# First expert weights issued ahead of the barrier, and one wait at the expert border removed

## Chip, cores and metric
The kernel runs on all 8 cores of one Trainium2 chip, each with one of the 8 sequences of the batch; the cores do not communicate. The metric is the device time in microseconds (us) of the slowest core.

## What is computed
One transformer layer with a parallel attention and expert branch, on x of shape 8 x 2048 x 1024 (float32):

```python
xn = layernorm(x)
x = x + local_attention(xn, w_qkv, b_qkv, w_proj, b_proj) + moe(xn, ...)

# local attention: 16 heads of 64, windows of 256 queries, keys of the
# window and of 128 positions on either side, softmax, projection
# moe: 8 experts, hidden size 2048, the best 2 of 8 weighted by softmax
h0 = einsum('td,ehd->eth', xt, w0) + b0
h1 = einsum('td,ehd->eth', xt, w1) + b1
out_all = einsum('eth,edh->etd', h0 * silu(h1), w2) + b2
out = (softmax(top_v) * take(out_all, top_i)).sum()
```

Every expert is computed for every token; a gate weight of zero drops the ones that are not chosen.

## The kernel before
Each core holds its 2048 tokens transposed: the 1024 features lie on partitions as 8 tiles `xn[dt]` of 128 x 2048 in bf16, the tokens run along the free dimension. All engines' instruction streams are written out by hand: `step` emits an instruction that may increment its engine's counter (`ct` TensorE, `cv` VectorE, `cs` ScalarE, `cg` GpSimd), `dma` emits a transfer that increments a counter of its own by 16, and `rec.wait` lets an engine wait until a counter has reached a value. `rec.wait` leaves out a wait on a value that the engine has already waited for. `barrier()` (L206) makes every engine drain, increment a counter of its own, and wait for those of the other four.

The stages come one after the other. Layer norm statistics, normalisation and gate; a barrier; the q, k and v projections; a barrier; the attention in 128 steps; a barrier; the transposes of the attention output (L660) and its projection (L681, evicted to the bf16 sum tiles `SUM[dt]` at L688). Then comes the b2 stage (L692 to L706): 32 rounds, each of one TensorE matmul of 8 x 128 by 8 x 512 (L699: the expert biases b2 times the gate weights) into one of two PSUM banks and one VectorE add into SUM (L704). Each matmul waits for the add of the round before it. After a further barrier (L711) the expert stage begins.

In the expert stage (L733 on) a loop runs over the 8 experts `e`. Its first part loops over 16 tiles `ht` of 128 hidden features, and for each over 4 token chunks `tc` of 512: eight matmuls with w0 (L756), eight with w1 (L762), the Silu on ScalarE (L771) and the product on VectorE into `act[ht]` (L777). PSUM banks 0 to 5 are used in turn as three pairs, so a chunk waits for the eviction three chunks before. The second part multiplies `act` by W2 (16 matmuls for each of 32 outputs, L798) into banks 6 and 7; VectorE multiplies by the gate weights `gwb` into `tmpb` (L803) and adds into SUM (L805).

The weights arrive from GpSimd's DMA queue (POOL in the profile), which converts them from float32 to bf16. `emit_slice_dma(e, ht)` loads the w0 and w1 slices of one `ht` (256 KB each) into one of four slots. For e = 0 the first four are issued before the loop's first matmul, followed by W2T of expert 0 (4 MB) and `gwb`. From then on a slot's next load is issued when its matmuls are done, so the first four slices of the next expert go out during the last four `ht` of this one. W2T of the next expert is issued after the last W2 matmul, its `gwb` after the last L805.

The memory for the slots, for W2T and for gwb overlaps `AO`, the attention output before its transposition, which the transposes read. `act` overlaps the transposed attention output and the projection weights.

At the top of every `ht` TensorE waits for its two slices and, where e > 0, for the last L805 of the expert before. `last_act`, which TensorE waits for between the two parts, covers all evictions of the PSUM pairs, and VectorE itself waits for the last W2 matmul before it writes `act` again. Behind the loop the final stage adds x and stores the result (L837).

Of the kernel before, what the change touches and what calls it, by code (L numbers as in the profile page):

```python
# [20 lines left out]
NDT = D // 128  # L21
NTT = T // 128
NTC = T // 512
# [33 lines left out]
def build_program(debug_upto=None):  # L57
# [8 lines left out]
    w2T_in = nc.dram_tensor("w2T", [NE, HF, D], F32, kind="ExternalInput")  # L66
# [9 lines left out]
    gw_hbm = nc.dram_tensor("gw_scratch", [NE, T], F32)  # L76
# [3 lines left out]
    def sb(name, shape, dtype, off):  # L80
        return nc.alloc_sbuf_tensor_at(name, shape, dtype, offset=base + off)
# [69 lines left out]
    W2T_sb = sb("W2T", [128, NHT * D], BF16, OB + 96 * KB)  # L151
    w0sl = [sb(f"w0sl{i}", [128, NDT * 128], BF16, OB + 128 * KB + i * 2 * KB) for i in range(4)]
    w1sl = [sb(f"w1sl{i}", [128, NDT * 128], BF16, OB + 136 * KB + i * 2 * KB) for i in range(4)]
    gwb_sb = sb("gwb", [128, T], BF16, OB + 144 * KB)
# [11 lines left out]
    rec = Rec()  # L166
    ct = Ctr(stack, nc, "ct")
    cv = Ctr(stack, nc, "cv")
# [9 lines left out]
    dgww = Ctr(stack, nc, "dgww")  # L178
    dw0 = [Ctr(stack, nc, f"dw0{i}") for i in range(4)]
    dw1 = [Ctr(stack, nc, f"dw1{i}") for i in range(4)]  # L180
    dw2 = Ctr(stack, nc, "dw2")
    dgwb = Ctr(stack, nc, "dgwb")
# [3 lines left out]
    def dma(eng, ctr, out_ap, in_ap):  # L186
        ctr.n += 16
        v = ctr.n
        sem = ctr.sem
        rec.emit(eng, lambda E, o_=out_ap, i_=in_ap, s=sem: E.dma_start(out=o_, in_=i_).then_inc(s, 16))  # L190
        return v
# [14 lines left out]
    def barrier():  # L206
        for e in Rec.ENGINES:
            c = BCTR[e]
            c.n += 1
            sem = c.sem  # L210
            rec.emit(e, lambda E, s=sem: E.drain().then_inc(s, 1))  # L211
        snap = {e: BCTR[e].n for e in Rec.ENGINES}
        for e in Rec.ENGINES:
            for f in Rec.ENGINES:
                if f != e:
                    rec.wait(e, BCTR[f], snap[f])
# [9 lines left out]
    def finalize():  # L226
        def run(E, name):
            for kind, f in rec.ops[name]:
                if kind == "op_dr":
                    E.drain()  # L230
                f(E)

        with nc.Block() as block:
            @block.tensor
            def _(t):
                run(t, "tensor")

            @block.vector
            def _(v):
                run(v, "vector")  # L240

            @block.scalar
            def _(s):
                run(s, "scalar")

            @block.sync
            def _(s):
                run(s, "sync")

            @block.gpsimd  # L250
            def _(g):
                run(g, "gpsimd")

        stack.close()
        return nc
# [210 lines left out]
    gwT_hbm_done = dma("sync", dgww, gw_hbm[:], gwT_sb[:])  # L466
# [203 lines left out]
    proj_mm = {}  # L670
# [37 lines left out]
    if debug_upto == "p3":  # L708
        finish_debug(SUM)
        return finalize()  # L710
    barrier()  # L711

    w2_loaded = 0
    gwb_loaded = 0
# [3 lines left out]
    w2_evac_d = {}  # L718
    b_last_mm = 0

    def emit_slice_dma(e, ht):
        slot = ht % 4
        if (e, ht - 4) in h_mm_done:
            rec.wait("gpsimd", ct, h_mm_done[(e, ht - 4)])
        elif e > 0 and ht < 4:
            rec.wait("gpsimd", ct, h_mm_done[(e - 1, NHT - 4 + ht)])
        a = dma("gpsimd", dw0[slot], w0sl[slot][:],
                w0T_in[e][:, ht * 128:(ht + 1) * 128].rearrange("(a p) o -> p a o", p=128))
        b = dma("gpsimd", dw1[slot], w1sl[slot][:],
                w1T_in[e][:, ht * 128:(ht + 1) * 128].rearrange("(a p) o -> p a o", p=128))  # L730
        sl_loaded[(e, ht)] = (slot, a, b)

    for e in range(NE):  # L733
        if e == 0:
            for _h in range(4):
                emit_slice_dma(0, _h)
            rec.wait("gpsimd", dgww, gwT_hbm_done)
            w2_loaded = dma("gpsimd", dw2, W2T_sb[:],
                            w2T_in[0][:, :].rearrange("(a p) d -> p a d", p=128))
            gwb_loaded = dma("gpsimd", dgwb, gwb_sb[:], gw_hbm[0][None, :].partition_broadcast(128))  # L740

        for ht in range(NHT):
            slot = ht % 4
            bcol = e * 16 + ht
            _sl, _a, _b = sl_loaded[(e, ht)]
            rec.wait("tensor", dw0[_sl], _a)
            rec.wait("tensor", dw1[_sl], _b)
            if e > 0:
                rec.wait("tensor", cv, w2_evac_d[(e - 1, NTC * NDT - 1)])
            for tc in range(NTC):  # L750
                i = ht * NTC + tc
                par = i % 3
                if i >= 3:
                    rec.wait("tensor", cv, act_evac[(e, i - 3)])
                for dt in range(NDT):
                    step("tensor", lambda t, s=slot, dt=dt, tc=tc, par=par: t.matmul(  # L756
                        pb[par * 2][:], w0sl[s][:, dt * 128:(dt + 1) * 128],
                        xn[dt][:, tc * 512:(tc + 1) * 512],
                        start=(dt == 0), stop=(dt == NDT - 1)))
                for dt in range(NDT):  # L760
                    last = (dt == NDT - 1)
                    h_mm_done[(e, ht)] = step("tensor", lambda t, s=slot, dt=dt, tc=tc, par=par: t.matmul(  # L762
                        pb[par * 2 + 1][:], w1sl[s][:, dt * 128:(dt + 1) * 128],
                        xn[dt][:, tc * 512:(tc + 1) * 512],
                        start=(dt == 0), stop=(dt == NDT - 1)), ct if last else None) \
                        or h_mm_done.get((e, ht), 0)
                hm = h_mm_done[(e, ht)]
                rec.wait("scalar", ct, hm)
                if i >= 3:
                    rec.wait("scalar", cv, act_evac[(e, i - 3)])  # L770
                sil_done = step("scalar", lambda s, par=par, bcol=bcol: s.activation(  # L771
                    out=silb[par][:], in_=pb[par * 2 + 1][:], func=AF.Silu,
                    bias=b1cols[:, bcol:bcol + 1], scale=1.0), cs)
                rec.wait("vector", cs, sil_done)
                if e > 0:
                    rec.wait("vector", ct, b_last_mm)
                act_evac[(e, i)] = step("vector", lambda v, ht=ht, tc=tc, par=par, bcol=bcol: v.scalar_tensor_tensor(  # L777
                    out=act[ht][:, tc * 512:(tc + 1) * 512], in0=pb[par * 2][:],
                    scalar=b0cols[:, bcol:bcol + 1], in1=silb[par][:],
                    op0=ALU.add, op1=ALU.mult), cv)  # L780
            if ht + 4 < NHT:
                emit_slice_dma(e, ht + 4)
            elif e + 1 < NE:
                emit_slice_dma(e + 1, ht + 4 - NHT)

        rec.wait("tensor", dw2, w2_loaded)
        rec.wait("vector", dgwb, gwb_loaded)
        last_act = act_evac[(e, NHT * NTC - 1)]
        rec.wait("tensor", cv, last_act)
        for tc in range(NTC):  # L790
            for dt in range(NDT):
                j = tc * NDT + dt
                bk = 6 + j % 2
                if j >= 2:
                    rec.wait("tensor", cv, w2_evac_d[(e, j - 2)])
                for ht in range(NHT):
                    last = (ht == NHT - 1)
                    b_last_mm = step("tensor", lambda t, ht=ht, dt=dt, tc=tc, bk=bk: t.matmul(  # L798
                        pb[bk][:], W2T_sb[:, ht * D + dt * 128:ht * D + dt * 128 + 128],
                        act[ht][:, tc * 512:(tc + 1) * 512],  # L800
                        start=(ht == 0), stop=(ht == NHT - 1)), ct if last else None) or b_last_mm
                rec.wait("vector", ct, b_last_mm)
                step("vector", lambda v, tc=tc, bk=bk, j=j: v.tensor_tensor(  # L803
                    tmpb[0][:], pb[bk][:], gwb_sb[:, tc * 512:(tc + 1) * 512], ALU.mult), dr=True)
                w2_evac_d[(e, j)] = step("vector", lambda v, dt=dt, tc=tc, j=j: v.tensor_tensor(  # L805
                    SUM[dt][:, tc * 512:(tc + 1) * 512], SUM[dt][:, tc * 512:(tc + 1) * 512],
                    tmpb[0][:], ALU.add), cv, dr=True)
        if e + 1 < NE:
            rec.wait("gpsimd", ct, b_last_mm)
            w2_loaded = dma("gpsimd", dw2, W2T_sb[:],  # L810
                            w2T_in[e + 1][:, :].rearrange("(a p) d -> p a d", p=128))
            rec.wait("gpsimd", cv, w2_evac_d[(e, NTC * NDT - 1)])
            gwb_loaded = dma("gpsimd", dgwb, gwb_sb[:],
                             gw_hbm[e + 1][None, :].partition_broadcast(128))
# [67 lines left out]
```

## Time and profile before
| | us |
|---|---|
| median of two runs | 3448.32 |
| the two runs | 3435.47 and 3461.17 |
| profiled execution | 3438.49 |
| its span (slowest core) | 3436.5 |
| spans of the 8 cores | 3423.9 to 3436.5 |

| engine | busy us | share of the span |
|---|---|---|
| TensorE (PE) | 3191.1 | 93% |
| VectorE (DVE) | 1066.8 | 31% |
| ScalarE (ACT) | 525.3 | 15% |
| GpSimd (POOL) | 272.8 | 8% |

The span runs from a core's first to its last instruction; the time of the execution holds a little more. PE stands for TensorE's matmuls, PEld for its weight loads, and an engine's name with a q (DVEq, POOLq) for its sequencer, which handles waits and semaphores. Matmuls are pipelined and their ends are modelled, so the time of a single one overlaps the next one's. In a row of the timeline, what stands in brackets is how long the engine was idle before and who ended that. L190 is the line of the helper `dma`. The granted clock is a share of TensorE's full 2.4 GHz.

### The profile page before, as it was taken

How to read it: one execution, taken by the hardware profiler on the slowest of the kernel's cores; microseconds unless marked ns; L12 is line 12 of the kernel's file. 1: busy time of each engine (PE TensorE's matmuls, PEld its weight loads, DVE VectorE, ACT ScalarE, POOL GpSimd, SP SyncE). 2: the span in 40 equal slices, each digit the busy share in tenths (PEclk: the TensorE clock that was granted, in tenths of full speed). 3: DMA queues.
4: the chain of work that ended last, by engine and by line, in shares of the span. 5: the costliest groups of instructions: out<-in, count | busy, mean ns of one | idle time of the engine just before them, and what ended most of it. 6: DMA issues, size and time to landing. Idle time of an engine off the chain costs nothing.

```text
span 3436.5 us, 38188 instructions; the slowest of 8 cores (3423.9 to 3436.5 us)
## 1 busy us (share of the span) xinstructions
PE 3191.1 (93%) x15278; PEld 1484.8 (43%) x15278; DVE 1066.8 (31%) x1816; ACT 525.3 (15%) x665; POOL 272.8 (8%) x303
## 2 busy tenths in 40 slices
PE   3689998689999999999999999999999999999993
PEld 0634554234444444444444444444444444444441
DVE  3533455412242223222322232233223322332233
ACT  2200473012101210111011001100120011001100
POOL 0010000021101110110011001100110011001001
PEclk6589656799999999999999999999999999999997
DMA  3233001084306330642163225313441443144204
GB/s 119 86 36 39 1 1 26 0 104 42 32 1 86 37 31 1 89 40 25 16 77 37 25 31 68 37 19 46 53 41 16 65 40 38 13 68 40 22 25 171
DMA packets 310573, 150.15 MB, mean 44 GB/s; under 512 B 285296, under 2 KB 287728, under 8 KB 306296
## 3 DMA queue, kind: packets, MB, share of 16 engines
q0 software_dynamic: 304016, 113.84, 29.4%
q10 hardware_dynamic: 2304, 16.78, 1.5%
q1 hardware_dynamic: 4080, 17.09, 1.4%
q8 instruction: 125, 2.05, 0.2%
q14 instruction: 48, 0.39, 0.0%
HBM read 252.53 MB, written 8.45 MB: 76 GB/s over the span
## 4 chain that ended last, share of the span: by engine, by line
PE 91%; DVE 3%; DMA 3%; issue 1%; ACT 1%; DVEq 1%; ACTq 0%; SPq 0%; POOL 0%; POOLq 0%
PE pd L756 26%; PE pb L798 26%; PE pd L762 26%; PE pd L585 3%; PE pd L499 2%; DMA xs<-xT 2%; PE pb L615 2%; PE pd L532 2%; PE pd L681 1%; PE pb L499 1%; DVE SUM L704 1%; PE pd L396 1%; PE pb L699 1%; DVEq L230 0%; PE pb L681 0%
## 5 line engine op out<-in xcount | busy, mean ns | idle before, releaser
L756 PE MATMUL pd<-xn,w0sl 128*128 128x512 bf16 x4096 | 969.0, 379 | 23.9 <-DVE SUM L805 12.3
L762 PE MATMUL pd<-xn,w1sl 128*128 128x512 bf16 x4096 | 967.6, 379 | 0.0
L798 PE MATMUL pb<-act,W2T 128*128 128x512 bf16 x4096 | 885.3, 379 | 14.7 <-DVE act L777 14.7
L777 DVE SCALAR_TENSOR_TENSOR act<-pd,b0cols,sil 128x512 bf16<-128x512 f32 x512 | 384.5, 751 | 1411.7 <-ACT sil L771 1411.7
L771 ACT ACTIVATE sil<-pd,b1cols 128x512 bf16<-128x512 f32 x512 | 351.9, 687 | 2213.2 <-PE pd L762 2213.2
L756 PEld LDWEIGHTS pd<-xn,w0sl 128*128 128x128 bf16 x4096 | 400.5, 98 | 510.0 <-issue 29.3
L798 PEld LDWEIGHTS pb<-act,W2T 128*128 128x128 bf16 x4096 | 400.2, 98 | 499.8 <-issue 18.4
L762 PEld LDWEIGHTS pd<-xn,w1sl 128*128 128x128 bf16 x4096 | 400.8, 98 | 483.4 <-issue 0.3
L803 DVE TENSOR_TENSOR tmpb<-pb,gwb 128x512 f32<-128x512 f32 x256 | 177.1, 692 | 525.5 <-PE pb L798 525.5
L190 POOL DMA_DIRECT2D w0sl<-w0T x128 | 112.1, 876 | 1640.3 <-PE pd L762 1511.9
L805 DVE TENSOR_TENSOR SUM<-SUM,tmpb 128x512 bf16<-128x512 bf16 x256 | 180.4, 705 | 19.6 <-issue 0.9
L598 ACT ACTIVATE exp<-pd,c_shift 128x1024 bf16<-128x1024 f32 (+1 forms) x128 | 135.7, 1062 | 252.1 <-PE pd L585 252.1
L585 PE MATMUL pd<-qT,kT 64*128 64x256 bf16 x480 | 123.4, 407 | 1.9 <-POOLq L211 1.9
L190 POOL DMA_DIRECT2D w1sl<-w1T x128 | 113.1, 883 | 0.0
L499 PE MATMUL pd<-xn,qksl 128*128 128x512 bf16 x384 | 95.5, 386 | 7.4 <-DMA qksl<-wqkvT 7.4
L615 PEld LDWEIGHTS pb<-V,exp 128*128 128x128 bf16 x960 | 55.3, 126 | 56.5 <-issue 56.5
L627 DVE TENSOR_SCALAR AO<-pb,rc 128x64 bf16<-128x64 f32 x256 | 72.6, 284 | 21.1 <-issue 1.4
L615 PE MATMUL pb<-V,exp 128*128 128x65 bf16 x960 | 73.9, 241 | 3.8 <-ACT exp L598 2.3
L190 POOL DMA_DIRECT2D W2T<-w2T x8 | 9.2, 1152 | 775.4 <-PE pb L798 775.4
L499 PEld LDWEIGHTS pd<-xn,qksl 128*128 128x128 bf16 x384 | 38.0, 99 | 54.6 <-issue 10.8
L625 DVE RECIPROCAL rc<-pb 128x1 f32<-128x1 f32 x256 | 41.6, 162 | 64.2 <-PE pb L615 64.1
L585 PEld LDWEIGHTS pd<-qT,kT 64*128 64x128 bf16 x480 | 49.0, 125 | 28.7 <-issue 2.4
(84 smaller groups left out, 743.7 us busy)
## 6 DMA issues: line engine op xcount, KB each, us to landing
w0sl<-w0T POOLq DMA_DIRECT2D x128, 256.0 KB, 4.4
w1sl<-w1T POOLq DMA_DIRECT2D x128, 256.0 KB, 5.2
W2T<-w2T POOLq DMA_DIRECT2D x8, 4096.0 KB, 30.8
xs<-xT SPq DMA_DIRECT2D x12, 1024.0 KB, 7.0
xs<-xT ACTq DMA_DIRECT2D x12, 1024.0 KB, 7.2
qksl<-wqkvT POOLq DMA_DIRECT2D x16, 256.0 KB, 4.8
gwb<-gw_scratch POOLq DMA_DIRECT2D x8, 512.0 KB, 32.2
outT<-ob ACTq DMA_DIRECT2D x4, 1024.0 KB, 5.0
```

The source lines that it names most:

```text
L190: rec.emit(eng, lambda E, o_=out_ap, i_=in_ap, s=sem: E.dma_start(out=o_, in_=i_).then_inc(s, 16))
L499: qk_mm_done[ot] = step("tensor", lambda t, s=slot, bs=bs, dt=dt, c=c: t.matmul(pb[bs + c][:], qksl[s][:, dt * 128:(dt + 1) * 128], xn[dt] ...
L585: dd = step("tensor", lambda t, d=dst, pt=pt, po=po, kt=kt, g=g: t.matmul(d, kT[pt][po:po + 64, kt * 128:(kt + 1) * 128], qT[pt][po:po + 6 ...
L598: exp_done_l[it] = step("scalar", lambda s, e=par, par=par, nk=nk: s.activation(out=expb[e][:, 0:nk * 256], in_=pd[par][:, 0:nk * 256], fu ...
L615: av_done = step("tensor", lambda t, e=par, j=j, qi=qi, kt=kt, abk=abk, h=h, nk=nk: t.matmul(pb[abk][:, qi * 65:qi * 65 + 65], expb[e][:, ...
L756: step("tensor", lambda t, s=slot, dt=dt, tc=tc, par=par: t.matmul(pb[par * 2][:], w0sl[s][:, dt * 128:(dt + 1) * 128], xn[dt][:, tc * 512 ...
L762: h_mm_done[(e, ht)] = step("tensor", lambda t, s=slot, dt=dt, tc=tc, par=par: t.matmul(pb[par * 2 + 1][:], w1sl[s][:, dt * 128:(dt + 1) * ...
L771: sil_done = step("scalar", lambda s, par=par, bcol=bcol: s.activation(out=silb[par][:], in_=pb[par * 2 + 1][:], func=AF.Silu, bias=b1cols ...
L777: act_evac[(e, i)] = step("vector", lambda v, ht=ht, tc=tc, par=par, bcol=bcol: v.scalar_tensor_tensor(out=act[ht][:, tc * 512:(tc + 1) * ...
L798: b_last_mm = step("tensor", lambda t, ht=ht, dt=dt, tc=tc, bk=bk: t.matmul(pb[bk][:], W2T_sb[:, ht * D + dt * 128:ht * D + dt * 128 + 128 ...
L803: step("vector", lambda v, tc=tc, bk=bk, j=j: v.tensor_tensor(tmpb[0][:], pb[bk][:], gwb_sb[:, tc * 512:(tc + 1) * 512], ALU.mult), dr=True)
L805: w2_evac_d[(e, j)] = step("vector", lambda v, dt=dt, tc=tc, j=j: v.tensor_tensor(SUM[dt][:, tc * 512:(tc + 1) * 512], SUM[dt][:, tc * 512 ...
```

## The change
Two edits. The first moves the barrier that stands between the b2 stage and the expert stage behind the first ten weight transfers, and takes these out of the loop over the experts. GpSimd now waits for the last projection matmul before it issues them; all transposes, which read the memory that they overwrite, come before that matmul. The second deletes TensorE's wait for the last L805 of the expert before.

```diff
     if debug_upto == "p3":
         finish_debug(SUM)
         return finalize()
-    barrier()
...
+    rec.wait("gpsimd", ct, proj_mm[NDT - 1])
+    for _h in range(4):
+        emit_slice_dma(0, _h)
+    rec.wait("gpsimd", dgww, gwT_hbm_done)
+    w2_loaded = dma("gpsimd", dw2, W2T_sb[:],
+                    w2T_in[0][:, :].rearrange("(a p) d -> p a d", p=128))
+    gwb_loaded = dma("gpsimd", dgwb, gwb_sb[:], gw_hbm[0][None, :].partition_broadcast(128))
+    barrier()
+
     for e in range(NE):
-        if e == 0:
-            for _h in range(4):
-                emit_slice_dma(0, _h)
-            rec.wait("gpsimd", dgww, gwT_hbm_done)
-            w2_loaded = dma("gpsimd", dw2, W2T_sb[:],
-                            w2T_in[0][:, :].rearrange("(a p) d -> p a d", p=128))
-            gwb_loaded = dma("gpsimd", dgwb, gwb_sb[:], gw_hbm[0][None, :].partition_broadcast(128))
-
         for ht in range(NHT):
...
             rec.wait("tensor", dw0[_sl], _a)
             rec.wait("tensor", dw1[_sl], _b)
-            if e > 0:
-                rec.wait("tensor", cv, w2_evac_d[(e - 1, NTC * NDT - 1)])
             for tc in range(NTC):
```

## Rows read from the trace of the kernel before

**Rows 1.** The cores: span and mean granted TensorE clock, the two longest.
```profile
core 3: 3435.6 us, clock 0.930
...
core 5: 3436.5 us, clock 0.931
```

**Rows 2.** The chain that ended last, by line, share of the span (page, part 4).
```profile
PE pd L756 26%; PE pb L798 26%; PE pd L762 26%; PE pd L585 3%; PE pd L499 2%; DMA xs<-xT 2%; PE pb L615 2%; PE pd L532 2%; PE pd L681 1%; PE pb L499 1%; DVE SUM L704 1%; PE pd L396 1%; PE pb L699 1%; DVEq L230 0%; PE pb L681 0%
```

**Rows 3.** Busy time by stretch, core 5: length, engines (instructions), clock, DMA share, GB/s.
```profile
640.00:690.00 50.00, 18.33 (x32) 3.18 (x32) 22.56 (x33) 0.00 (x0) 0.00 (x0) 0.52 0.00 0
690.00:700.00 10.00, 0.00 (x0) 0.00 (x0) 0.00 (x0) 0.00 (x0) 8.68 (x10) 0.50 0.81 68
700.00:704.00 4.00, 3.55 (x10) 1.34 (x11) 0.00 (x0) 0.00 (x0) 0.00 (x0) 0.58 1.45 133
704.00:925.00 221.00, 219.16 (x1016) 99.25 (x1015) 48.07 (x64) 45.31 (x65) 27.68 (x32) 1.00 0.56 62
925.00:1037.30 112.30, 110.55 (x512) 49.91 (x511) 44.31 (x64) 0.00 (x0) 1.49 (x2) 1.00 0.05 5
```

**Rows 4.** Waits of core 5: engine line <- releaser: total us, times, longest.
```profile
PE pd L756 <- DVE SUM L805: 12.3, 7, 1.8
PE pd L756 <- DMA w1sl<-w1T: 11.6, 1, 11.6
```

**Rows 5.** Timeline of core 5, 630 to 726 us: start, us, engine, line, operation.
```profile
637.13 0.59 PE L681 MATMUL pb<-AOT,wp 128*128 128x512 bf16 x2
...
641.37 0.69 DVE L704 TENSOR_TENSOR SUM<-SUM,pb 128x512 bf16<-128x512 bf16 x1 [0.80 <-PE pb L699]
...
688.98 0.69 DVE L704 TENSOR_TENSOR SUM<-SUM,pb 128x512 bf16<-128x512 bf16 x1 [0.83 <-PE pb L699]
690.38 0.87 POOL L190 DMA_DIRECT2D w0sl<-w0T  x1 [128.41 <-DVEq L211]
...
698.42 0.63 POOL L190 DMA_DIRECT2D gwb<-gw_scratch  x1
...
700.45 3.31 PE L756 MATMUL pd<-xn,w0sl 128*128 128x512 bf16 x8 [11.58 <-DMA w1sl<-w1T]
```

**Rows 6.** Timeline of core 5 at the first border between experts.
```profile
1029.78 5.78 PE L798 MATMUL pb<-act,W2T 128*128 128x512 bf16 x26
...
1036.11 1.15 POOL L190 DMA_DIRECT2D W2T<-w2T  x1 [110.77 <-PE pb L798]
1036.48 0.69 DVE L805 TENSOR_TENSOR SUM<-SUM,tmpb 128x512 bf16<-128x512 bf16 x1
...
1037.32 1.89 PE L756 MATMUL pd<-xn,w0sl 128*128 128x512 bf16 x8 [1.76 <-DVE SUM L805]
```

**Rows 7.** Chain that ended last, core 5, 636 to 712 us: start, us, what.
```profile
689.67 0.06 DVEq L211
...
691.24 9.08 DMA w1sl<-w1T
...
703.76 1.73 PE pd L762 x8
```

**Rows 8.** The same chain on core 3.
```profile
689.71 7.86 DMA w1sl<-w1T
...
697.70 3.57 PE pd L756 x8
701.28 2.65 PE pd L762 x8
```

**Rows 9.** DMA issues of core 5, 690 to 746 us, KB each, us to landing.
```profile
W2T<-w2T POOLq DMA_DIRECT2D x1, 4096.0 KB, 45.6
...
gwb<-gw_scratch POOLq DMA_DIRECT2D x1, 512.0 KB, 47.1
```

**Rows 10.** Timeline of core 5 after the last W2 matmul.
```profile
3383.86 4.07 POOL L837 TENSOR_TENSOR ob<-SUM,xs 128x2048 f32<-128x2048 bf16 x1 [165.68 <-PE pb L798]
3384.57 3.91 DVE L805 TENSOR_TENSOR SUM<-SUM,tmpb 128x512 bf16<-128x512 bf16 x1
```

## Prediction

> **What bounds the kernel now.** I read the cores first. Core 5 is the slowest with 3436.5 us and core 3 is next with 3435.6 [rows 1]. The profiled execution took 3438.49 us, so 1.99 us lie outside the span. All sums below are made against that execution. The runs shown are 3435.47 and 3461.17 us with a median of 3448.32, so the profiled execution lies near the lower one and 9.8 us under the median.
>
> Then the chain that ended last, by line: the three expert matmul lines L756, L762 and L798 hold 26% each [rows 2]. TensorE is the bound. From 704 us on it is busy 219.16 of 221 us and its granted clock is 1.00, the 2.4 GHz level [rows 3]. Inside the expert stage there is thus little to win except where TensorE stands still. There are two such places that this change can touch, and the waits of the chain name both: 11.6 us once, for the DMA into w1sl, and 12.3 us in 7 waits, for the add of L805 [rows 4].
>
> The first place is the seam between the b2 additions and the experts. On core 5 the last projection matmul ends near 637.72 (637.13 + 0.59). From then to 689.67 TensorE and VectorE take turns, one small matmul and one L704 add at a time: 32 adds, the first at 641.37, the last at 688.98, 1.54 us apart. Only when the barrier has passed does POOL issue its ten DMAs, the first at 690.38, the last at 698.42. The first expert matmul starts at 700.45 [rows 5]. During the b2 stage no DMA moves anything: its share is 0.00 [rows 3].
>
> The second place is each of the 7 borders between experts: after the last W2 matmul, VectorE multiplies (L803) and adds (L805), and only then does L756 of the next expert start, at 1037.32 [rows 6].
>
> **The change, step by step.**
>
> *The DMAs move ahead of the barrier.* POOL now waits for the last projection matmul in place of VectorE's last b2 add. The second wait that moves with them, for the gate weights stored to HBM long before, costs nothing. Four pairs of slices, W2T and gwb, ten issues in all, then start about 0.6 us after 637.72, at 638.3; the 0.6 us is taken from 690.38 - 689.73, release to first issue [rows 5, 7]. They occupy POOL for 8.68 us (in the stretch 690 to 700, as now [rows 3]), so until about 647. The first pair, which landed 9.08 us after the second issue began [rows 7], is there by about 648.5, some 41 us before it is wanted. The load is fully hidden behind the b2 stage; if that cover were gone, the 11.6 us would be back.
>
> What is behind the DMAs on POOL's queue is only the barrier, which POOL reaches at about 647, and VectorE at 689.7. So VectorE still ends the barrier last. TensorE then finds its slices. VectorE's barrier semaphore is at 689.73 and POOL's release needs a few steps of 0.06 us; from data landed (700.32) to matmul took 0.13 us [rows 5, 7]. I take 0.5 us from VectorE's end, so the first L756 stands at 690.2. The gain on core 5 is 700.45 - 690.2 = 10.3 us (10.0 to 10.6). On core 3 the second issue began 1.53 us earlier (689.71 against 691.24) and the first L756 at 697.70 [rows 7, 8], so its barrier ends at 688.14 + 0.5 and its gain is 9.1 us.
>
> The clock at the start: the b2 stage has 0.52, near the 1.2 GHz level, though TensorE is busy for 18.33 of 50 us. The first 4 us of the experts have 0.58 [rows 3], so the first eight matmuls take 3.31 us, and those after them 1.73. After the change the stage before is the same, so I price this start as now. Core 3 needed 2.65 us for its second eight [rows 8], which bounds the uncertainty at about 0.9 us either way.
>
> W2T and gwb land 45.6 and 47.1 us after issue [rows 9]; they are first read at 925, now and then. Earlier landing is worth nothing there. Slices of ht = 4 and later, which now queue behind W2T, only get more room.
>
> *The wait for L805 goes.* Eight full matmuls take 1.73 us of the chain [rows 7], so starts are 0.216 us apart, and the last of the 26 that begin at 1029.78 starts at 1029.78 + 25 x 0.216 = 1035.18. The next starts at 1037.32 [rows 6]: 2.14 us where 0.216 would do. That is 1.92 us at each of 7 borders, 13.5 us. The lower bound is nothing, if another wait takes its place. What would be late next? The next expert's first four slice pairs wait only for this expert's last L762, so they have the 110 us of the W2 matmuls [rows 3] to land. The banks of par 0 to 2 were emptied before W2 began. The fourth tile's wait for act comes three tiles (6 x 1.73 = 10.4 us) later, and VectorE is through with L805 at 1037.17, before the first tile's own matmuls (two times 1.73 us from 1035.4) have ended. So nothing is late, and I take 13.5.
>
> *Does POOL's work disturb the b2 stage?* Before, POOL was idle in it, so no row shows an L704 beside a DMA issue. The nearest: an L805, which has two operands in SBUF, ran 0.69 us from 1036.48 while POOL issued W2T from 1036.11 to 1037.26 [rows 6]; that price is nothing. The farthest: the last L805 took 3.91 us in place of 0.69, beside a POOL tensor operation that began at 3383.86 and lasted 4.07 [rows 10]. So POOL can hold VectorE up. If each of the ten issues did so in full, the b2 stage would grow by 8.7 us. I take nothing, since the first row has the same kind of POOL instruction.
>
> The Trainium skill, "SBUF — State Buffer", section "SBUF: two separate sides", says that VectorE and GpSimd share a port pair under an exclusive lock, which the first to start keeps for its whole instruction. The last L805 agrees with it, the one beside W2T does not show it for a DMA issue. By the lock applied to issues the sum would be 8.7 us worse, by the row nothing.
>
> *Sum.* Core 5: 3436.5 - 10.3 - 13.5 = 3412.7. Core 3: 3435.6 - 9.1 - 13.5 = 3413.0, which makes it the slowest by a little. With 1.99 outside the span: **3415 us**, 23.5 us or 0.7% less than the profiled execution. The end of the kernel (stores and adds) moves with it unchanged.
>
> **The rivals.**
>
> *POOL's barrier waits for its transfers.* The barrier begins with a drain, and no row shows POOL draining with transfers of its own under way. If the drain held until gwb landed, then by the present course (first issue 690.38, gwb at 698.42 + 47.1 = 745.5, 55.1 us together [rows 5, 9]) POOL would be free at 693.4, and the first L756 would start at 693.9: a gain of 6.5 in place of 10.3, 3419 us. It decides only above 52 us from first issue to last landing. Against it: POOL issues the next DMA without waiting for the one before [rows 5].
>
> *VectorE is held up in the b2 stage*, as priced above: 3415 + 8.7 = 3424 us. The row beside W2T speaks against it.
>
> *The change doesn't do what it says at one place.* If another wait takes the place of L805, 3415 + 13.5 = 3428.5; if the first slices still come late, 3415 + 10.3 = 3425. I found no candidate for either.
>
> *Slower: TensorE's clock gives back more than is won.* The place is the expert stage, 700 to 3384 us. Its matmuls scale with the clock, so each 0.01 of granted clock costs about 27 us there; at a loss of 0.009 the 23.5 us are gone, and at 0.99 in place of 1.00 the time would be 3442. For it: the same kernel has a run that is 25.7 us longer than the other, so something of this size does occur, though no row shows what; and the change takes away the only pauses of the stage. Against it: the pauses are 1.76 us [rows 6] in some 333 (221.0 + 112.3), and the stretch of 221 us without one has 1.00 [rows 3].
>
> **How the numbers follow.** Both gains as worked out: 0.74, time 3415, its own range 3411 to 3419. Drain: 0.07, at 3419. VectorE held up: 0.06, at 3424. One part without effect: 0.07, at 3425 to 3428.5. Clock: 0.06, at 3442. The runs before lie 3 us below and 23 us above the profiled one, so one that catches the upper spread may read 3438. The range goes from 3408 (the likeliest's low end less the 3 us) to 3436: it takes in all but the clock case and part of that spread, about 0.15. A difference of 2%, 69 us, is about what a measurement of this kernel can tell from no change. No case wins 69 us, as both idle times together are 24, so faster has 0.01. The clock would have to fall by over 0.03 for slower, 0.02. Within 2%: 0.97.
>
> **What the profile after would show.** If right: POOL's first w0sl issue near 638, no wait of L756 for a DMA, first L756 within 1 us of the last L704, no wait of L756 for L805, and starts 0.22 us apart at the borders. L704 keeps 0.69 us and its rounds 1.54. A longer L704 or longer rounds would show VectorE held up. A POOL semaphore as the last releaser of the barrier, well behind VectorE's end, would show the drain. A granted clock under 1.00 inside the experts would show the last rival. The prediction is wrong if TensorE, freed at either place, stands still in front of something I did not list.

## The result

The kernel after takes 3419.73 us against 3440.49 before (medians of 18 and 17 runs). The ratio of the comparable runs is 0.9929, with a 95% interval of 0.9911 to 0.9948: a gain of 0.5 to 0.9%, clear of noise and within 2%. The profiled execution took 3416.62 us. Some runs of both kernels were much longer, with a lower granted clock on one die or both; they are in these two medians, and in no ratio or comparison of runs below, which use the others, called comparable. Thirteen runs of each kernel are left. Those after lie between 3414.8 and 3422.0 us; eleven of those before lie between 3435.5 and 3443.6, and two apart, at 3461.17 and 3470.83. Without these two the ratio of the means is 0.9941.

The spans of the two longest cores after, which answer to [rows 1] (core: span and mean granted clock):

```profile
core 3: 3414.2 us, clock 0.930
...
core 7: 3414.5 us, clock 0.930
```

The waits of core 7 on TensorE's first expert line are short now. Of the two rows in [rows 4] neither is left; one new wait has come:

```profile
PE pd L756 <- POOLq L211: 5.0, 1, 5.0
```

POOLq L211 is GpSimd's sequencer in the barrier's drain, the instruction that `barrier()` begins with on every engine. The wait of 11.6 us for w1sl has become one of 5.0 us for POOL, and the 12.3 us for L805 have gone without a successor. The seam on core 7, which answers to [rows 5] (timeline: start, us, engine, line, operation):

```profile
632.05 0.87 POOL L190 DMA_DIRECT2D w0sl<-w0T  x1 [76.29 <-PE pb L681]
...
640.10 0.63 POOL L190 DMA_DIRECT2D gwb<-gw_scratch  x1
...
682.75 0.69 DVE L704 TENSOR_TENSOR SUM<-SUM,pb 128x512 bf16<-128x512 bf16 x1 [0.83 <-PE pb L699]
...
687.61 3.20 PE L756 MATMUL pd<-xn,w0sl 128*128 128x512 bf16 x8 [4.97 <-POOLq L211]
```

The issues begin behind the projection, as forecast, and end about 640.7. The last b2 add ends at 683.44, but the first expert matmul starts 4.17 us later. The chain of the same core shows what held it, which answers to [rows 7] (start, us, what):

```profile
636.42 50.81 POOLq L211
687.23 0.38 issue
687.61 3.20 PE pd L756 x8
690.81 1.73 PE pd L762 x8
```

POOL's sequencer is on the chain until 687.23. The last of its transfers to land, gwb, took 46.6 us from 640.10, so it landed at about 686.7, half a microsecond before (DMA issues of core 7, KB each, us to landing; they answer to [rows 9]):

```profile
W2T<-w2T POOLq DMA_DIRECT2D x1, 4096.0 KB, 45.3
...
gwb<-gw_scratch POOLq DMA_DIRECT2D x1, 512.0 KB, 46.6
```

On core 2 of the same execution gwb was issued at 637.95 and took 42.4 us, so it landed at 680.35, before the last add's end at 681.07. There VectorE is the last releaser, and the first expert matmul starts 0.72 us after the add's end:

```profile
681.79 3.57 PE L756 MATMUL pd<-xn,w0sl 128*128 128x512 bf16 x8 [1.52 <-DVEq L211]
```

On five of the eight cores POOL is the last releaser, as on core 7, and on three VectorE, as on core 2.

The border between experts on core 7, which answers to [rows 6]. The 59 matmuls begin at 1009.70, so the last starts at 1009.70 + 58 x 0.216 = 1022.23, and L756 follows 0.21 us later, without a gap:

```profile
1009.70 12.90 PE L798 MATMUL pb<-act,W2T 128*128 128x512 bf16 x59
1022.44 1.89 PE L756 MATMUL pd<-xn,w0sl 128*128 128x512 bf16 x8
```

Busy time by stretch on core 7, which answers to [rows 3] (length, busy us of PE, PEld, DVE, ACT and POOL with instructions, granted clock, DMA share, GB/s):

```profile
634.00:683.40 49.40, 18.35 (x32) 3.17 (x32) 22.28 (x33) 0.00 (x0) 6.73 (x8) 0.52 1.10 136
683.40:687.60 4.20, 0.00 (x0) 0.02 (x1) 0.03 (x1) 0.00 (x0) 0.00 (x0) 0.50 0.14 27
687.60:692.00 4.40, 4.39 (x15) 1.74 (x16) 0.00 (x0) 0.00 (x0) 0.00 (x0) 0.69 0.00 0
692.00:908.00 216.00, 216.00 (x1003) 97.91 (x1002) 46.95 (x63) 44.58 (x64) 26.24 (x30) 1.00 0.38 37
...
692.00:3362.00 2670.00, 2650.52 (x12275) 1200.25 (x12273) 741.75 (x1025) 353.14 (x513) 232.68 (x263) 1.00 0.34 38
```

The transfers now lie under the b2 stage (136 GB/s where there was 0), the stage itself has the same clock of 0.52, the first expert matmuls start at a lowered clock as before (0.69 over 4.4 us), and from 692 to 908 TensorE is busy all the time. Its clock is 1.00 there and over the whole expert stage.

To see where the time went, I cut every core's span at four points of its timeline and took the mean over the 8 cores: the first L704 starts; the last L704 ends; the first expert matmul starts; the last L803 starts. "Seam" is the third stretch, "tail" what follows the last point. Each row comes from one profiled execution of a kernel.

| us, mean of 8 cores | to the b2 stage | b2 stage | seam | experts | tail |
|---|---|---|---|---|---|
| before | 636.43 | 48.21 | 8.78 | 2683.84 | 52.63 |
| after | 634.55 | 48.18 | 2.10 | 2670.34 | 53.66 |
| move_only | 638.08 | 48.14 | 1.44 | 2683.75 | 54.62 |
| wait_only | 636.27 | 48.13 | 9.02 | 2670.42 | 54.12 |
| slices_ahead | 637.52 | 48.14 | 0.73 | 2670.28 | 54.77 |
| signal_first | 635.41 | 48.21 | 0.74 | 2670.09 | 55.32 |
| after_b2two | 637.19 | 24.45 | 24.42 | 2670.62 | 54.58 |
| half_w2_b2two | 636.11 | 24.41 | 11.61 | 2670.68 | 52.61 |
| signal_first_b2two | 636.51 | 24.45 | 0.73 | 2670.14 | 53.79 |

The change won 13.50 us in the experts and 6.68 in the seam. The first and the last column, whose work no edit touches, differ by up to 3.5 and 2.7 us between these executions; on single cores the b2 stage begins anywhere from 630 to 644 us. That is noise for the question here, and it is as large as some of the terms. So differences of a few us are read from the seam and the experts, and the times only say how they add up.

### The profile page after: what moved, and what is told of

Same layout as the page of the kernel before. It is cut to its first block, busy times and chain, and to the rows that moved or that the text cites. A ratio compares the mean times of both kernels' runs of the same rounds, so it can differ in the third digit from the quotient of the medians.

```text
span 3414.5 us, 38182 instructions; the slowest of 8 cores (3402.2 to 3414.5 us)
## 1 busy us (share of the span) xinstructions
PE 3190.9 (93%) x15278; PEld 1485.5 (44%) x15278; DVE 1066.5 (31%) x1816; ACT 525.2 (15%) x665; POOL 272.8 (8%) x303
## 4 chain that ended last, share of the span: by engine, by line
PE 91%; DVE 2%; DMA 2%; POOLq 1%; issue 1%; ACT 1%; DVEq 1%; POOL 0%; ACTq 0%; SPq 0%
PE pd L756 26%; PE pb L798 26%; PE pd L762 26%; PE pd L585 3%; PE pd L499 2%; DMA xs<-xT 2%; PE pb L615 2%; PE pd L532 2%; POOLq L211 1%; PE pd L681 1%; PE pb L499 1%; PE pd L396 1%; DVEq L230 0%; PE pb L681 0%; DVE st_d L350 0%
## 5 line engine op out<-in xcount | busy, mean ns | idle before, releaser
L756 PE MATMUL pd<-xn,w0sl 128*128 128x512 bf16 x4096 | 968.9, 379 | 5.0 <-POOLq L211 5.0
L762 PE MATMUL pd<-xn,w1sl 128*128 128x512 bf16 x4096 | 967.6, 379 | 0.0
L798 PE MATMUL pb<-act,W2T 128*128 128x512 bf16 x4096 | 885.3, 379 | 14.7 <-DVE act L777 14.7
L798 PEld LDWEIGHTS pb<-act,W2T 128*128 128x128 bf16 x4096 | 400.2, 98 | 499.8 <-issue 18.4
L756 PEld LDWEIGHTS pd<-xn,w0sl 128*128 128x128 bf16 x4096 | 401.0, 98 | 489.4 <-issue 7.1
L762 PEld LDWEIGHTS pd<-xn,w1sl 128*128 128x128 bf16 x4096 | 400.8, 98 | 483.3 <-issue 0.2
L803 DVE TENSOR_TENSOR tmpb<-pb,gwb 128x512 f32<-128x512 f32 x256 | 177.0, 691 | 525.6 <-PE pb L798 525.6
L805 DVE TENSOR_TENSOR SUM<-SUM,tmpb 128x512 bf16<-128x512 bf16 x256 | 180.4, 705 | 19.6 <-issue 0.9
```

## The experiments

**Theory.** POOL's drain in the barrier does not end before the last transfer that POOL itself has issued has landed. The moved barrier therefore waits for VectorE's last add or for gwb, whichever is later. **Rivals.** The gain lies in the removed wait alone; POOL is held by its ten issues as such, by a fixed cost, or by the b2 work; the running transfer itself, not the drain, holds TensorE.

**One part alone: the move.** The changed kernel with TensorE's wait for L805 put back:

```diff
             rec.wait("tensor", dw1[_sl], _b)
+            if e > 0:
+                rec.wait("tensor", cv, w2_evac_d[(e - 1, NTC * NDT - 1)])
```

> The barrier and the ten DMAs moved as in the change, but TensorE keeps its wait for L805 at the borders. Drain theory (POOL's drain in the barrier ends only when its last transfer, gwb, has landed): the 7 waits of L756 for L805 are back with 12.3 us in all, the first L756 starts as in the changed kernel, on most cores behind POOL's sequencer 2.5 to 5 us after VectorE's end. Time = changed kernel + 13.5 = about 3433 us, 6 to 7 us under the kernel before. Rival (the moved barrier brings nothing, the whole gain is the removed wait): about 3440, as before.

Its one comparable run took 3433.67 us, where 3433 was expected; with a single run there is no interval. The profile speaks more clearly. The waits of the first expert line, here L758 (core 0):

```profile
PE pd L758 <- DVE SUM L807: 12.3, 7, 1.8
...
PE pd L758 <- POOLq L211: 2.8, 1, 2.8
```

The 12.3 us are back, the experts take 2683.75 us as before, and the seam keeps its gain (1.44 us against 8.78). The move does pay by itself. POOL is the last releaser on five of the eight cores here too, but there the first expert matmul comes 1.3 to 2.7 us after VectorE's end, where 2.5 to 5 was expected.

**The other part alone: the wait.** The kernel before, without the wait for L805:

```diff
-            if e > 0:
-                rec.wait("tensor", cv, w2_evac_d[(e - 1, NTC * NDT - 1)])
```

> Only TensorE's wait for L805 removed, barrier and DMAs where they were before. By the sum of the prediction 7 x 1.92 = 13.5 us: about 3427 us, no wait of L756 for L805, L756 still waits 8 to 12 us for w1sl. Rival (another wait takes the place of L805): within 3 us of the kernel before, and a new wait of L756 of about 1.8 us, 7 times.

Its comparable runs lie at 3423.3 to 3430.3 us, ratio 0.9962 (0.9947 to 0.9976), and the experts take 2670.42 us, 13.42 less than before. The first expert line (here L754; core 4) has one wait left, the old one:

```profile
PE pd L754 <- DMA w1sl<-w1T: 11.5, 1, 11.5
```

No other wait took the place of L805. The two parts add up: 13.4 us in the experts here, 7.3 in the seam with the move alone, 20.2 together in the kernel after.

**Fewer transfers ahead of the barrier.** W2T and gwb go behind it, the eight slices stay ahead:

```diff
+    barrier()
     rec.wait("gpsimd", dgww, gwT_hbm_done)
     w2_loaded = dma("gpsimd", dw2, W2T_sb[:],
                     w2T_in[0][:, :].rearrange("(a p) d -> p a d", p=128))
     gwb_loaded = dma("gpsimd", dgwb, gwb_sb[:], gw_hbm[0][None, :].partition_broadcast(128))
-    barrier()
```

> As the changed kernel, but only the eight slice DMAs are issued ahead of the barrier; W2T and gwb follow behind it. Drain theory: POOL's drain ends when the last slice has landed, 10 to 20 us after its issue, long before VectorE's end; VectorE is the last releaser on all cores, first L756 0.7 us after the last L704 ends, which gains 3 to 4 us on the slowest cores: 3415 to 3417 us against 3419.7. Rival (POOL is held by the issuing of ten DMAs as such, or PE's first slices are late): first L756 stays 3 to 5 us behind VectorE's end on the slowest cores and the time at 3419 to 3420.

VectorE releases the barrier on all 8 cores and the seam is 0.72 to 0.76 us everywhere. Core 7:

```profile
PE pd L756 <- DVEq L211: 1.5, 1, 1.5
```

Its comparable runs lie at 3415.4 to 3418.5 us, ratio 0.9934 (0.992 to 0.9948). That is not told apart from the kernel after; the seam's 1.4 us are too little for the times to show. POOL's own drain can be read as well (core 7: the last issue, and the record of the drain with count, duration in ns min/median/max, and start):

```profile
642.44 0.94 POOL L190 DMA_DIRECT2D w1sl<-w1T  x1
```

```profile
L211 POOLq DRAIN  x1: 15667/15667/15667, 639.7 to 639.7; - x1
```

It ends at 655.4, 12.0 us after the last of the eight issues and 0.4 us after the last slice landed (654.99), so here too it is the landing and not the issuing that it follows. But this run changes two things, how many are issued and how long they run.

**All ten transfers, and the drain ahead of them.** The barrier is split: every engine drains and signals, then POOL issues its ten DMAs, then all wait for the signals. The transfers are those of the kernel after:

```diff
+    bar_snap = barrier_signal()
     rec.wait("gpsimd", ct, proj_mm[NDT - 1])
     for _h in range(4):
         emit_slice_dma(0, _h)
...
-    barrier()
+    barrier_wait(bar_snap)
```

> As the changed kernel, with all ten DMAs before the expert stage, but POOL drains and increments its barrier counter before it issues them, and waits for the other engines behind them. Drain theory: no engine waits for POOL any more although the same ten transfers are under way until about 686 us; VectorE is the last releaser on all cores, first L756 0.7 us after the last L704 ends, time 3415 to 3417 us. Rival (the running 4 MB transfer itself, not the drain, holds TensorE's start, for example through the semaphores or the memory): first L756 stays 3 to 5 us behind VectorE's end, 3419 to 3420 us.

On all cores VectorE is the last releaser and the seam 0.72 to 0.76 us, also where gwb was still on its way. On core 7 gwb was issued at 642.17 and took 45.4 us, so it landed at 687.57. The first expert matmul (L762) had started 1.64 us before:

```profile
642.17 0.63 POOL L190 DMA_DIRECT2D gwb<-gw_scratch  x1
...
685.93 3.36 PE L762 MATMUL pd<-xn,w0sl 128*128 128x512 bf16 x8 [1.55 <-DVEq L211]
```

The same issues, the same transfers, no hold: it was the drain behind them. The expectation of the time was missed. The comparable runs lie at 3417.3 to 3421.1 us, ratio 0.994 (0.9926 to 0.9954), no faster than the kernel after (3414.8 to 3422.0). In its profile the tail is 1.7 us longer in the mean, more than the 1.4 us that the seam gives; that is within the noise of the tail, and no run here shows a cause.

**A shorter cover.** In the next three kernels a b2 matmul waits for the add two rounds back, which the two banks allow:

```diff
-            rec.wait("tensor", cv, max(gwTb_done, b2_evac, proj_evac[NDT - 1]))
+            rec.wait("tensor", cv, max(gwTb_done, b2_prev, proj_evac[NDT - 1]))
...
+            b2_prev = b2_evac
             b2_evac = step("vector", lambda v, dt=dt, c=c, bk=bk: v.tensor_tensor(
```

First the kernel after with this alone:

> The changed kernel with a shorter b2 stage: a b2 matmul waits for the add two rounds back in place of the last one, as there are two banks. Two rounds in flight should cut the stage from 48.2 us to about 25. Drain theory (POOL's drain holds the barrier until gwb has landed): the barrier is held by POOL on all 8 cores until about 0.5 us after gwb's landing, so the stage's saving turns into a wait of L756 of some 20 to 25 us for POOL's sequencer, and the time stays near the changed kernel: 3416 to 3421 us. Rival (POOL is held by something tied to VectorE's or TensorE's b2 work and not by its transfers): the barrier follows the end of the b2 stage, 3395 to 3400 us.

The b2 stage falls from 48.2 to 24.5 us, and the seam grows from 2.1 to 24.4. The ratio is 0.994 (0.9921 to 0.996), from two comparable runs of 3416.70 and 3420.67 us: no faster than without the shorter stage. Core 0:

```profile
644.53 0.63 POOL L190 DMA_DIRECT2D gwb<-gw_scratch  x1
...
691.31 3.57 PE L758 MATMUL pd<-xn,w0sl 128*128 128x512 bf16 x8 [28.19 <-POOLq L211]
```

and its DMA row and chain:

```profile
gwb<-gw_scratch POOLq DMA_DIRECT2D x1, 512.0 KB, 45.9
```

```profile
640.84 50.08 POOLq L211
```

gwb lands at 644.53 + 45.9 = 690.43, POOL's drain ends at 690.92. Of the 23.7 us that the stage lost, 22.3 went into the wait for POOL. POOL is the last releaser on all 8 cores, and the seam is 22.0 to 27.4 us, a little over the 20 to 25 expected.

**Half of the data.** As the last one, but only 2 of W2T's 4 MB go ahead of the barrier:

```diff
-    w2_loaded = dma("gpsimd", dw2, W2T_sb[:],
-                    w2T_in[0][:, :].rearrange("(a p) d -> p a d", p=128))
+    dma("gpsimd", dw2, W2T_sb[:, 0:8 * D],
+        w2T_in[0][0:1024, :].rearrange("(a p) d -> p a d", p=128))
     gwb_loaded = dma("gpsimd", dgwb, gwb_sb[:], gw_hbm[0][None, :].partition_broadcast(128))
     barrier()
+    w2_loaded = dma("gpsimd", dw2, W2T_sb[:, 8 * D:16 * D],
+                    w2T_in[0][1024:2048, :].rearrange("(a p) d -> p a d", p=128))
```

> As the kernel with the short b2 stage, but only half of W2T (2 of 4 MB) goes ahead of the barrier, then gwb; the other half follows behind the barrier. Drain theory: the hold shortens with the data on the way; gwb lands some 14 to 20 us earlier (about 27 to 32 us after its issue in place of 41 to 47), and POOL releases the barrier about 0.5 us behind that, so the first L756 comes 14 to 20 us earlier after the first b2 add than with all of W2T. Rival (a fixed cost of POOL's drain or of the issues): release at the same distance as with all of W2T.

Core 0, the issue, the DMA row and the chain:

```profile
643.72 0.63 POOL L190 DMA_DIRECT2D gwb<-gw_scratch  x1
```

```profile
gwb<-gw_scratch POOLq DMA_DIRECT2D x1, 512.0 KB, 32.9
```

```profile
640.31 36.80 POOLq L211
```

gwb lands at 676.62, the drain ends at 677.11. The distance is 0.49 us again, as with all of W2T, while the hold is 13.28 us shorter. In the mean the seam falls from 24.42 to 11.61 us. That is 12.8 us where I had expected 14 to 20: the direction is the theory's, the saving that I had estimated was too large. Its one run took 3402.65 us.

**The short stage with the drain ahead.** The split barrier and the two rounds in flight together:

> The short b2 stage together with POOL signalling the barrier before its transfers. Drain theory: VectorE releases the barrier, first L756 0.7 us after the last b2 add on all cores, so the 23 us of the stage are won in full: 3394 to 3399 us, ratio to the kernel before about 0.987. Rival (the running transfers hold TensorE or VectorE in another way, e.g. the first slices land too late for a stage of 25 us, or the adds grow longer beside POOL's issues): less than half of it, 3405 us or more.

The comparable runs lie at 3391.2 to 3395.1 us, ratio 0.987 (0.9851 to 0.989). The seam is 0.73 us in the mean, VectorE the last releaser on all cores, and the 23.7 us of the b2 stage are won in full. On core 1 gwb lands 45.7 us after its issue, at 692.24, and the experts (L764) have been running for 25.7 us by then:

```profile
646.54 0.63 POOL L190 DMA_DIRECT2D gwb<-gw_scratch  x1
...
666.52 3.32 PE L764 MATMUL pd<-xn,w0sl 128*128 128x512 bf16 x8 [1.52 <-DVEq L211]
```

This version beats both kernels: by 1.3% the one before, and by about 0.7% the one after, whose thirteen comparable runs average 3418.7 us where these three average 3393.4. Neither of its two parts was faster than the kernel after by itself.

## Why the prediction was right, and where not

*The time.* 3415 was forecast, from 3408 to 3436, and 3419.73 measured; the gain of 23.5 us came out as 20.8 between the medians of all runs, and as 21.9 between the two profiled executions. Both gains came from the two places that were named; the rest of the kernel moved only within its noise.

*The wait for L805.* 7 x 1.92 = 13.5 us was forecast; the experts shrank by 13.50, with the move and (13.42) without it. The rival that another wait takes its place is out: no wait follows at the borders.

*The step that failed: "So VectorE still ends the barrier last."* It was argued from POOL having done with its issues at about 647. POOL was done with them about then, counted from its start, but its drain was not: it ended half a microsecond behind gwb's landing. The seam's gain was forecast as 10.3 and 9.1 us on the two slowest cores, which leaves a seam of 0.5. The seam was 2.10 us in the mean and 4.17 on core 7; where VectorE was last it was 0.72, so the 0.5 itself was 0.2 short. The rival "POOL's barrier waits for its transfers", held at 0.07, is what happened. It was priced at 3419, from 55.1 us between first issue and last landing; on core 7 these are 686.70 - 632.05 = 54.7. The argument against it, that POOL issues the next DMA without waiting for the one before, says nothing about a drain. The prediction's premise that no row shows POOL draining with transfers of its own under way holds for the rows it shows, but not for the trace they came from. At 561 us on core 5, right behind the issue of the projection weights (wp), POOL drains for the barrier in front of the experts. This is the kernel before (timeline, DMA issue with KB and us to landing, and the record of the drain with its duration in ns):

```profile
561.08 0.88 POOL L190 DMA_DIRECT2D wp<-wprojT  x1 [275.15 <-ACTq L211]
```

```profile
wp<-wprojT POOLq DMA_DIRECT2D x1, 2048.0 KB, 15.3
```

```profile
L211 POOLq DRAIN  x1: 15399/15399/15399, 561.1 to 561.1; - x1
```

The issue is over at 561.96, wp lands at 576.38, and the drain ends at 576.46. Two earlier drains of POOL end in the same way, 0.21 and 0.29 us behind the landing of its last transfer, and one with nothing under way takes 0.05 us. Nothing waited for these drains, so they cost nothing before. With these rows the rival deserved far more than 0.07. What it cost hung on a few us: on the eight cores after, 49 to 55 us lie between POOL's first issue and gwb's landing, and 51 between that issue and VectorE's end.

*The rest of the distance.* The sum was made against 3438.49, and the median before over 17 runs is 2.0 us above that. The hold of 3.5 us on the slowest core (4.17 - 0.7) and these 2.0 are a little more than the 4.7 us between 3415 and 3419.73; the noise of the start and the tail does not let single us be told apart. That the time stayed inside the range is thus no support for the seam's forecast, whose error of 3.5 us is small in a range of 28, and that 3419.73 stands so near the 3419 of the rival is in part luck.

*VectorE held up in the b2 stage.* It was not. On core 7 the first four of the 32 adds, from 635.13 on, ran before the last issue ended at 640.73. No add took longer than 0.689 us, where before, without issues, the longest took 0.690 (duration in ns, min/median/max, core 7):

```profile
L704 DVE TENSOR_TENSOR SUM<-SUM,pb x32: 686/686/689, 635.1 to 682.7; 128x512 bf16<-128x512 bf16 x32
```

The stage took 48.18 us against 48.21. What the Trainium skill, "SBUF — State Buffer", section "SBUF: two separate sides", tells of the lock between VectorE and GpSimd is seen in [rows 10] for a tensor operation (L805 took 3.91 us there, in place of 0.69), and is not seen here for DMA issues beside an add with one operand in SBUF and one in PSUM. For a VectorE operation outside the 2-port modes the section names as the lock's condition two SBUF inputs, beside a GpSimd operation that reads SBUF; the last L805 has two, L704 one.

*The clock.* 1.00 in the experts of the kernel after, without the pauses at the borders. The slower rival did not occur. The prediction called these the only pauses of the stage, which they are not: before each expert's second part TensorE waits 1.8 us for the last product in `act`, in both kernels alike, and the stage's clock is 1.00 all the same (the wait on core 5 before: us in total, times, longest):

```profile
PE pb L798 <- DVE act L777: 14.7, 8, 1.8
```

The slow start of the experts stayed: a clock of 0.69 over the first 4.4 us, eight matmuls in 3.20 us.

## What to carry to other kernels

Where GpSimd loads weights ahead of a barrier that begins with a drain, expect the barrier to wait for those weights, as here: let GpSimd signal first and issue then, or keep what is not wanted at once behind the barrier. Such a signal no longer covers the transfers, so their readers must wait for the transfers' own counters, as they do in this kernel. Before calling a case unseen, look in the trace of before for every record of the instruction in question. Count the cover of an early load to the last landing on that engine, not to the end of its issues. A wait that other waits already imply can cost its full turn-round at every pass. Here that was 1.92 us at 7 borders, and removing it won 13.50 us because nothing else was late behind it.

## What was not expected of the hardware

GpSimd's drain ended 0.48 to 0.49 us after the landing of gwb, the last transfer that GpSimd had issued, on all 8 cores of the four kernels that drain behind it (after, move_only, after_b2two, half_w2_b2two; 4.5 or 6.5 MB on the way). The drains lasted 32 to 51 us, although each issue had occupied GpSimd for 0.6 to 1.2 us only. With other last transfers the distance was 0.08 us (wp), 0.21, 0.29 or 0.41 us; what sets it, no run here shows. Transfers of other engines are not waited for: on core 5 before, the first drain ended at 10.51 us, while one of SyncE's landed at 14.59 and one of ScalarE's at 18.24. So W2T held the experts by the drain alone: its data were first read some 225 us later (L798 at 911.93 on core 7 after).
